# Linear attention with queries moving: packed summaries as the stationary operand, attended tiles left on feature rows

## What is computed

```python
def _feature_map(x):
    return jnp.where(x > 0, x + 1.0, jnp.exp(x))
q = query @ Wq.T
gate = jax.nn.sigmoid(query @ Wg.T + bg)
k, v = jnp.split(kv @ Wkv.T, 2, axis=-1)          # 16 heads of 32 features
q, k = _feature_map(q), _feature_map(k)
kv_summary = jnp.einsum('bhsd,bhse->bhde', k, v)
k_sum = k.sum(axis=-2)
z = 1.0 / (jnp.einsum('bhld,bhd->bhl', q, k_sum)[..., None] + EPS)
attn = jnp.einsum('bhld,bhde->bhle', q, kv_summary) * z
out = attn * gate @ Wo.T
```

## Time and profile before

| | |
|---|---|
| median of 3 runs | 1021.06 us (1021.02 to 1021.27) |
| profiled execution, its own time | 1021.25 us |
| its span in the trace | 1019.6 us |
| TensorE busy | 1006.6 us, 99% |
| VectorE busy | 694.4 us, 68% |
| ScalarE busy | 597.2 us, 59% |
| GpSimd busy | 281.5 us, 28% |
| mean granted TensorE clock | 0.998 of full speed |

### The profile page before, as it was taken

The page is one execution under the profiler, slowest core; times in us unless marked ns, Lnnn a source line. Parts: engine busy times, 40 slices in busy tenths (PEclk is TensorE's granted clock), DMA queues, the critical chain, the costliest instruction groups (busy, mean ns, idle before and its releaser), DMA issues.

```text
span 1019.6 us, 16277 instructions
## 1 busy us (share of the span) xinstructions
PE 1006.6 (99%) x5738; PEld 802.1 (79%) x5738; DVE 694.4 (68%) x1371; ACT 597.2 (59%) x953; POOL 281.5 (28%) x444
## 2 busy tenths in 40 slices
PE   8999999999999999999999999999999999999996
PEld 6888888886455555578888888888888999999996
DVE  6758555538999998678777775677724566666662
ACT  6776788747889998874333344111204466666662
POOL 1022222125655553110000034100010154455542
PEclk9999999999999999999999999999999999999999
DMA  6693666522010000301111342302063688888863
GB/s 232 244 338 119 186 185 198 165 73 85 22 31 23 22 21 1 98 18 63 62 64 52 105 134 84 120 10 83 1 199 121 216 232 229 225 242 252 238 158 46
DMA packets 50339, 127.29 MB, mean 125 GB/s; under 512 B 5856, under 2 KB 9952, under 8 KB 49504
## 3 DMA queue, kind: packets, MB, share of 16 engines
q1 hardware_dynamic: 39248, 97.79, 28.7%
q0 software_dynamic: 10448, 27.58, 11.6%
q10 hardware_dynamic: 576, 1.05, 0.3%
HBM read 98.02 MB, written 28.38 MB: 124 GB/s over the span
## 4 chain that ended last, share of the span: by engine, by line
PE 73%; DVE 1%; issue 0%; ACT 0%; POOL 0%; DVEq 0%; ACTq 0%
PE bank L56 17%; PE bank L57 17%; PE bank L58 17%; PE bank L1500 9%; PE bank L1521 5%; PE bank L2459 1%; PE bank L1512 1%; PE bank L1581 1%; PE bank L1599 1%; PE bank L1530 1%; PE bank L1568 0%; PE bank L2446 0%; PE bank L2429 0%; PE bank L2430 0%; PE bank L1624 0%
## 5 line engine op out<-in xcount | busy, mean ns | idle before, releaser
L1500 PE MATMUL bank<-w,f_qT 128*128 128x512 bf16 x512 | 118.0, 379 | 0.5 <-DVE f_h L1796 0.5
L2281 POOL DMA_INDIRECT out<-e_y,scatter_idx x32 | 69.0, 2157 | 109.4 <-ACT e_y L2388 89.5
L1500 PEld LDWEIGHTS bank<-w,f_qT 128*128 128x128 bf16 x512 | 48.4, 98 | 51.5 <-issue 1.1
L2264 POOL DMA_INDIRECT e_xg<-xn_rows,gather_idx x32 | 32.1, 1004 | 162.3 <-DVE gather_idx L2667 96.7
L2319 ACT ACTIVATE s_m_h<-s_mid 128x512 fp32r<-128x512 f32 (+1 forms) x24 | 15.2, 632 | 105.1 <-DVE s_mid L2677 59.0
L2785 DVE TENSOR_TENSOR e_mid<-bank,e_sil 128x256 f32<-128x256 f32 (+1 forms) x47 | 19.7, 420 | 59.2 <-ACT e_sil L2358 59.2
L1521 PE MATMUL bank<-w,f_q2T 128*128 128x512 bf16 x256 | 57.9, 379 | 0.3 <-ACT f_q2T L1227 0.3
L1796 DVE SCALAR_TENSOR_TENSOR f_h<-bank,f_columns,f_sg 128x512 f32<-128x512 f32 x64 | 47.9, 749 | 10.9 <-PE bank L1500 5.3
L56 PE MATMUL bank<-e_xT_h,e_wg_h 128*128 128x256 f32 (+1 forms) x192 | 55.2, 287 | 0.0
L57 PE MATMUL bank<-e_xT_l,e_wu_h 128*128 128x256 f32 (+1 forms) x192 | 54.1, 282 | 0.0
L56 PE MATMUL bank<-e_xT_h,e_wu_h 128*128 128x256 f32 (+1 forms) x192 | 54.0, 281 | 0.0
(11 more groups left out here) (466 smaller groups left out, 3301.6 us busy)
## 6 DMA issues: line engine op xcount, KB each, us to landing
wraw<-in_wffn SPq DMA_DIRECT2D x48, 512.0 KB, 4.2
e_raw_g<-in_ew_gate SPq DMA_DIRECT2D x16, 704.0 KB, 4.1
e_raw_u<-in_ew_up SPq DMA_DIRECT2D x16, 704.0 KB, 5.4
e_raw_d<-in_ew_down SPq DMA_DIRECT2D x16, 512.0 KB, 6.5
sorted_y<-e_y SPq DMA_DIRECT2D x19, 256.0 KB, 4.1
x_rows<-rows SPq DMA_DIRECT2D x16, 256.0 KB, 2.0
xn_rows<-a_work SPq DMA_DIRECT2D x16, 256.0 KB, 2.0
s_raw<-x_rows SPq DMA_DIRECT2D x16, 256.0 KB, 2.6
```

Of the source, the lines that this page charges most:

```text
L1500: ins = pe.matmul(bank[c % 2][:, :], qT[t % 2][:, k * P:(k + 1) * P], w_gv(k, col + c * 512), start=(k == 0), stop=(k == KD - 1))
L2264: gp.indirect_dma_start(xg[t][u][:, :], None, g.xn_dram, bass.IndirectOffsetOnAxis(g.gather_idx[:, slot:slot + 1], 0)).then_inc(e_arrived[ ...
L2281: gp.indirect_dma_start(io["out"], bass.IndirectOffsetOnAxis(g.scatter_idx[:, slot:slot + 1], 0), e_y[t][u][:, :], None, compute_op=ALU.ad ...
```

## The change

The queries now move. For each unit n (chunk n%4 of batch n//4) `attend(n)` issues four matmuls with 512 columns, all with the features on the rows of the result. A packed summary (`pack_summary`, two additions on POOL) has in the first 64 columns of a chunk the values of its heads 0 and 1, on those heads' rows, and the key sums of heads 2 and 3 on theirs, and in the other 64 the reverse. So bank 0 gets in its upper 64 rows the numerators of heads 0 and 1 and in its lower 64 the denominators of heads 2 and 3, each of them repeated over 32 rows. SP loads it three times over, as `summ_top`, `summ_bottom` and `summ_low`, with five DMAs a batch. The query tile holds the high part and the low part of one half of the heads above each other, so one matmul of 128 rows does two of the three products, and a second one of 64 rows does the third.

ACT copies the denominators of both banks into one tile; DVE turns them in 32x32 blocks, inverts one value of each block, spreads it by a second block turn, multiplies by the gate, and multiplies both banks by the result. The gate has the weights stationary and the tokens moving, its bias is a column that ACT adds. No attended tile is turned on PE. Low parts of queries and attended tiles are now taken on POOL. The order on all engines is written anew with four tables. In the front stage and for the last batch the packing sits on POOL between the making of the summary and its splitting; the splitting of the last batch's summary moves from turn 0 of the feed-forward's loop to turns 1 (ACT) and 2 (DVE).

```diff
+def pack_summary(gp, packed, summ, packed_part):
+
+    pairs = P // HD // 2
+    for cols, first in ((UPPER, pairs), (LOWER, 0)):
+        gp.tensor_tensor(packed[:, :, cols].rearrange("p k (h d) -> p k h d", d=HD), summ[:, :, cols].rearrange("p k (h d) -> p k h d", d=HD),
+                         summ[:, :, P + first:P + first + pairs].unsqueeze(3).to_broadcast([P, KD, pairs, HD]), ALU.add).then_inc(packed_part, 1)
...
+        ASKED = {0: 4, 1: 5, 2: 6, 3: 7, 6: 8, 7: 9, 8: 10, 9: 11, 10: 12, 11: 13, 12: 14, 13: 15}
+        PROJECTED = {4: (0,), 5: (1, 2), 6: (3,), 8: (4,), 9: (5, 6), 10: (7,), 12: (8,), 13: (9,), 14: (10,), 15: (11,)}
+        TURNED_ROWS = {5: (0,), 6: (1, 2), 7: (3,), 9: (4,), 10: (5, 6), 11: (7,), 13: (8,), 14: (9,), 15: (10,)}
+        ROUTED_ROWS = {6: (0,), 7: (1, 2), 8: (3,)}
...
             @block.sync
-                    if s in (2, 6, 10):
-                        sp.wait_ge(n_ready, s + 2)
+                    if s in (0, 4, 8):
+                        sp.wait_ge(n_ready, 2 * (s + 4))
                         summaries(s // 4 + 1)
...
             @block.gpsimd
+                def low_query(n):
+                    gp.wait_ge(feature_hi, CT + n + 1)
+                    first, second = two(n)
+                    gp.tensor_tensor(first[LOWER, :], e[n % 2][UPPER, :], f(first[UPPER, :]), ALU.subtract).then_inc(first_low, 1)
+                    gp.wait_ge(first_low, n + 1)
+                    gp.tensor_tensor(second[UPPER, :], e[n % 2][LOWER, :], f(second[LOWER, :]), ALU.subtract).then_inc(feature_lo, 1)
+                    gp.wait_ge(feature_lo, CT + n + 1)
+
+                def low_attended(n):
+                    gp.wait_ge(aT_hi, n + 1)
+                    high, low = two(n)
+                    gp.tensor_tensor(low, att[:, :], f(high), ALU.subtract).then_inc(aT_lo, 1)
...
+                gp.wait_ge(shift2_ready, TT)
+                for n in range(KD):
+                    low_query(n)
+                for n in range(TT):
+                    if n - 1 in ASKED:
+                        low_query(ASKED[n - 1])
+                    low_attended(n)
+                    for s in PROJECTED.get(n, ()):
+                        row_scale(s)
...
             @block.scalar
+                    first, second = two(n)
+                    act.activation(first[UPPER, :], e[n % 2][UPPER, :], ACT.Copy)
+                    act.activation(second[LOWER, :], e[n % 2][LOWER, :], ACT.Copy).then_inc(feature_hi, 1)
...
+                def denominators(n):
+                    if n:
+                        act.wait_ge(weight_ready, n)
+                    act.wait_ge(n_ready, 2 * n + 1)
+                    act.activation(den[UPPER, :], nbank[0][LOWER, :], ACT.Copy, bias=2 * ATT_EPS, scale=2.0).then_inc(den_ready, 1)
+                    act.wait_ge(n_ready, 2 * n + 2)
+                    act.activation(den[LOWER, :], nbank[1][UPPER, :], ACT.Copy, bias=2 * ATT_EPS, scale=2.0).then_inc(den_ready, 1)
...
                 split_q(2)
                 query(3)
+                tanh(0)
                 split_x(TT - 1)
+                for k in range(KD):
+                    split_w(2, k)
...
+                for n in range(TT):
+                    if n:
+                        tanh(n)
+                    denominators(n)
+                    turned = TURNED_ROWS.get(n, ())
+                    if n - 1 in ASKED:
+                        phi(ASKED[n - 1])
+                    for s in turned[:1]:
+                        a_split_x(s)
+                    if n - 1 in ASKED:
+                        split_q(ASKED[n - 1])
+                    split_att(n)
+                    for s in turned[1:]:
+                        a_split_x(s)
...
             @block.tensor
+                def attend(n):
+                    b, c = unit(n)
+                    if c == 0:
+                        pe.wait_ge(summ_in, 5 * 16 * (b + 1))
+                    if n:
+                        pe.wait_ge(att_ready, n)
+                    else:
+                        pe.wait_ge(feature_ready, CT + KD)
+                    pe.wait_ge(feature_lo, CT + n + 1)
+                    for x, bank, both, r in zip(two(n), nbank, (summ_top, summ_bottom), (UPPER, LOWER)):
+                        pe.matmul(bank[:, :], both[:, c, :], x, start=True, stop=False)
+                        pe.matmul(bank[:, :], summ_low[r, c, :], x[r, :], start=False, stop=True).then_inc(n_ready, 1)
...
+                def project(s):
                     b, t = s // 4, s % 4
                     if t == 0:
+                        pe.wait_ge(aT_lo, KD * (b + 1))
                     if s:
                         pe.wait_ge(x3_ready, s)
...
+                for n in range(TT):
+                    attend(n)
+                    if n + 1 < TT:
+                        gate(n + 1)
+                    turned, projected = TURNED_ROWS.get(n, ()), PROJECTED.get(n, ())
+                    for s in projected[:1]:
+                        project(s)
+                    for s in turned[:1]:
+                        a_turn_x(s)
+                    for s in projected[1:]:
+                        project(s)
+                    if n in ASKED:
+                        query(ASKED[n])
+                    for s in turned[1:]:
+                        a_turn_x(s)
+                    for s in ROUTED_ROWS.get(n, ()):
+                        route(s)
...
+                project(EARLY)
+                a_turn_x(EARLY - 1)
+                project(EARLY + 1)
...
             @block.vector
+                def attended(n):
+                    v.wait_ge(den_ready, 2 * n + 2)
+                    v.transpose(den_turned, den).then_inc(den_sorted, 1)
+                    v.wait_ge(den_sorted, n + 1)
+                    v.reciprocal(z[:, :], den_turned[:, 0:S:HD]).then_inc(z_ready, 1)
+                    v.wait_ge(z_ready, n + 1)
+                    v.transpose(den.rearrange("p (j d) -> p j d", d=HD), z[:, :].unsqueeze(2).to_broadcast([P, S // HD, HD])).then_inc(z_spread, 1)
+                    v.wait_ge(z_spread, n + 1)
+                    v.wait_ge(th_ready, n + 1)
+                    v.scalar_tensor_tensor(out=th[:, :], in0=th[:, :], scalar=1.0, in1=den, op0=ALU.add, op1=ALU.mult).then_inc(weight_ready, 1)
+                    v.wait_ge(weight_ready, n + 1)
+                    if n:
+                        v.wait_ge(aT_hi, n)
+                        v.wait_ge(aT_lo, n)
+                    v.tensor_tensor(att[UPPER, :], nbank[0][UPPER, :], th[UPPER, :], ALU.mult)
+                    v.tensor_tensor(att[LOWER, :], nbank[1][LOWER, :], th[LOWER, :], ALU.mult).then_inc(att_ready, 1)
...
+                for n in range(TT):
+                    for s in PROJECTED.get(n - 1, ())[-1:]:
+                        a_normalise(s)
+                    if n - 1 in ASKED:
+                        phi(ASKED[n - 1])
+                    attended(n)
+                    turned, projected = TURNED_ROWS.get(n, ()), PROJECTED.get(n, ())
+                    for s in turned[:1]:
+                        a_split_x(s)
+                    for s in projected[:-1]:
+                        a_statistics(s)
+                        a_normalise(s)
+                    for s in projected[-1:]:
+                        a_statistics(s)
```

More of the change, by code:

```diff
@@ L151, in front_experts0 @@
     summ = low.take("summ", [P, KD, SW], fp32)
-    summ_h, summ_l = [low.take(n, [P, KD * SW], f32r) for n in ("summ_h", "summ_l")]
+    summ_h, summ_l = [low.take(n, [P, KD * P], f32r) for n in ("summ_h", "summ_l")]
     assert low.at <= g.kept_at
@@ L1268, in tanh @@
[L1268 to L1284 removed]
+                        act.wait_ge(ao_ready, 4 * (b - 1))
@@ L1425, in _ @@
+                a_split_x(EARLY - 1)
+                shared["split_w"](0)
+                shared["split_w"](1)
+                a_split_x(EARLY)
+                turned_logits(2)
+                shared["split_w"](2)
+                a_split_x(EARLY + 1)
+                batch_logits(2)
+                shared["split_w"](3)
+                a_split_x(EARLY + 2)
+                logits(EARLY)
+                shared["split_w"](4)
+                shared["split_w"](5)
                 act.wait_ge(x3_out, 16 * EARLY)
@@ L1434, in _ @@
                 shared["split_w"](9)
-                a_split_x(TT - 1)
-                logits(TT - 2)
+                logits(TT - 1)
                 shared["activate"](2)
+                shared["softmax"]()
                 act.wait_ge(feature_lo, CT + TT)
@@ L1572, in attend @@
-                    last.then_inc(n_ready, 1)
-                def turn_att(s):
-                    pe.wait_ge(att_ready, s + 1)
-                    if s:
-                        pe.wait_ge(aT_lo, s)
-                    else:
-                        pe.wait_ge(feature_ready, CT + KD + 2)
-                    for k in range(KD):
```

(4 more changed lines are left out.)

405 lines of the change are left out of this document (142 added, 263 removed).

## The result

The changed kernel took 1077.6 us in the median of 5 runs (1072.7 to 1079.9), the kernel before 1021.1 (1020.6 to 1022.4, 5 runs): 5.5% slower, ratio 1.0547 with an interval of 1.0528 to 1.0566. The forecast was 1052, the range 1036 to 1065. The sign was right, the size 26 us short, outside the range. The profiled execution was the fastest of the five, 1072.68 us; its mean granted clock was 0.980, that of the other four 0.973 to 0.976. The kernel before spread over 1.7 us, this one over 7.

What follows compares the result with a forecast made beforehand. PE was taken to bound the kernel: -10.8 us of its work and waits of +10.1, +9.8, +4.6, +11.4, +4.3 and +2.3 made +31.7, less about 1 for overlaps +31, hence 1052 us, range 1036 to 1065.

Steps and rivals of the forecast that it cites:

- What bounds it: Whole kernel: PE, busy 99% of the span, sets the time; the change is worth PE's saved work less its new waits.
- PE's work: PE's own list: 16 attends and their transposes, 25.3 us, give way to 64 matmuls of 512 columns, 14.5 us: -10.8 us.
- The ring: Steps 1 to 4: attend(n+1) waits for att_ready(n), 8.8 us apart; 2.1 us before attend(2) to (5), 0.3 before five gates: +10.1.
- The start: First steps: waits of 3.0 us before turn_x(15), 2.9 before attend(0), 1.0 before gate(1), 2.9 before attend(1): +9.8.
- project(2) and (6): Those two projections: only one transpose separates them from the product whose bank DVE empties; 2.3 us wait each, +4.6.
- Low parts: From step 7: late low query parts from POOL delay attend(11), (12), (14), (15), and logits and a gate by 1.2 us: +11.4.
- project(12): After attend(15): the projection waits for the low part of the last attended tile, 7.3 us against 3.1 of work: +4.3.
- The end: Last four projections, one transpose between each, and the logits copied behind ACT's table load: +2.3 us.
- The clock: Within a rival of chance 0.12: long PE gaps bring the 1.2 GHz level three or four times, 8 to 11 us more, 1061.
- C: Rival, chance 0.12: longer chains, block turns at 1.35 us, +13 to 1065; or clock drops after long gaps, 1061.
- A: Main case, chance 0.62: PE's saved work and the listed waits come as forecast, 1044 to 1060 us.
- D: Rival, chance 0.10: the att_ready chain closes inside PE's work, POOL's low parts too; PE keeps all 10.8 us, 1010.5.

Runs made afterwards that it cites:

- e_full: Changed kernel with low summaries on all 128 rows, zeros in the unused half, so no matmul of attend uses 64 rows; 1063.3 us median.
- e_ring: Changed kernel with, in steps 1 to 4, the attended tile handled before the query's phi and split on DVE, ACT and POOL; 1070.0 us median.
- the best order: Changed kernel with full-height summaries and the work of ACT, DVE and POOL reordered twice; 1049.1 us median.

## Why the prediction fell short

- **What bounds it**: right. PE's list, its waits and its clock are the whole account; the front stage moved nothing.
- **PE's work, -10.8**: this is the first step that failed. The text took the full price from a row of 96 rows by 512 columns that "lasts 389 ns as the full ones do". That row tells a duration, not a distance, and as a neighbour 96 rows don't behave as 64 do: those matmuls follow at 0.23 like full ones, also where they meet 128 rows. The 64 matmuls cost 27.4 us instead of 14.5 at the full clock, and the gates 1.8 more. e_full shows it: the distances go back to 0.24, `attend` and the gates give about 12 us. I even named an end below (4 us at most to gain) and none above.
- **The ring, +10.1**: the chain was right (phi, turn 0.70, weight up to 1.59), the distance from attend to attend 9.2 us; the waits before attend(2) to (5) were 5.8 instead of 8.4 (the text's terms, 4 x 2.1 and 5 x 0.3, make 9.9) and no gate waited, since PE's own part had grown by 0.8 and in one step by the clock.
- **The start, +9.8**: 3.3 and 2.3 for 3.0 and 2.9; gate(1) did not wait, and attend(1) 0.3 instead of 2.9, because PE spent that time at the lower clock. Measured 5.8.
- **project(2) and (6), +4.6**: 4.0. **Low parts, +11.4**: 1.5, 1.9, 1.6, 4.7 for 1.7, 2.0, 1.7, 4.8, and 0.4 for 1.2: 10.1. **project(12), +4.3**: 2.6; its terms add up to 6.95, not 7.3, so the text's own reading gives 3.9. **The end, +2.3**: 2.0.
- **The clock**: the second step that failed, and it was not in the sum at all. The text put it in a rival, "three or four times", "8 to 11", and only behind gaps of 3 us and more. There were six drops and 13.5 us in the fastest run and, going by the clock of the others (0.973 to 0.976 against 0.980) and their times, about 5 us more in the median. Four of the six came behind gaps of 1.5 to 1.9, and the forecast's own list had nine gaps of 1.7 to 2.3.
- **Together**: 14.6 for the rows, 13.5 for the clock, 5 more of it in the median and 3.6 of small distances are 36.7 us that the sum did not have; the waits were 11 smaller than in it. That leaves the 26 us by which the forecast was short. The 11 are no merit of the forecast: the two missing terms filled time in which PE was to wait.
- **Rivals**: C's mechanism came true on top of A, not in its place. D needed a ring inside PE's work; e_ring reached that in steps 1 to 5, but the start and the later steps kept their waits, and the best order came down to 20 us of them. Treating the clock as an alternative to the waits, when most of it follows from them, is why the range ended at 1065.

## What to carry to other kernels

Price a matmul by the distance between starts in a row with the same neighbours; where operands of 64 and of 128 rows alternate, expect that each change exposes the weight load, and fill up the low ones with zeros or group them. If a forecast has PE, until then without a gap, wait more than ten times in 200 us, as here, the lower clock belongs in the sum and not among the rivals. And before work is taken off a saturated engine, ask what the order of the others can keep up with: here every wait removed uncovered another, and 10.8 us of work was never worth the ring.

## What the runs showed of the hardware that was not expected

- Start to start 0.43 us at the full clock and 0.72 at the lower one, where 64-row and 128-row matmuls with 512 columns alternate; 0.24 and 0.43 in one height. Two 64-row matmuls on different halves of the rows, one behind the other, ran at the same time (0.50 for both, 0.58 to the next one).
- The 1.2 GHz level came behind gaps of 1.5 to 1.9 us that repeat at 10 to 16 us, and in three kernels behind one of 0.4 among narrow routing matmuls; in one execution a lone gap of 2.8 us did not bring it and one of 4.1 did. A low stretch lasted 3 to 10 us, waits in it included, and cost 1.3 to 3.6. The runs of a kernel differ in their mean clock, and the spread grew from 2 us to 7 and more.
- Matmuls whose results nobody reads made the kernel 10.6 us faster in the median.
